# GpSimd adds the identity to the second-next adapter's first tiles one step later, behind the following slot's low parts and mixing matrices

## The reference, cut to what matters

```python
x = x + einsum('bct,bcd->bdt', x, W0[cond])        # x is (32, 64, 1024) f32
x = x + einsum('bct,bcd->bdt', x, W1[cond])        # 64x64 mixings over the sequence
x = x + base(x, W) + low_rank(x, lora[labeler])    # 1024x1024, and rank 32
w = weight[adapter_ids]                            # 8 adapters of 1024x1024, ids 3..7 drawn
x = x + einsum('bsi,boi->bso', x, w)
```

## Time and profile before

| | us |
|---|---|
| median of three runs | 383.75 (383.16 to 384.0) |
| the profiled execution | 384.77 |
| its span, from the first to the last instruction | 383.0 |
| TensorE busy in the span | 376.4 (98%) |
| VectorE busy | 267.6 (70%) |
| ScalarE busy | 225.5 (59%) |
| GpSimd busy | 115.3 (30%) |

### The profile page before, as it was taken

One profiled execution on the slowest core, in us unless ns is written; L12 is line 12 of the kernel. 1 busy time (PEld: TensorE's weight loads), 2 busy tenths in 40 slices (PEclk: granted clock), 3 DMA queues, 4 the chain that ended last, 5 costly groups with the idle time before them and its releaser, 6 DMA issues.

```text
span 383.0 us, 7652 instructions
## 1 busy us (share of the span) xinstructions
PE 376.4 (98%) x1733; PEld 312.9 (82%) x1734; DVE 267.6 (70%) x301; ACT 225.5 (59%) x299; POOL 115.3 (30%) x157
## 2 busy tenths in 40 slices
PE   8999999999999999999999999999999999999995
PEld 7888888888888888888888888778888888888784
DVE  3796977847849788447968458844599635999653
ACT  3689577487247375244474565753677536778443
POOL 0000230100000000024765356663167532566600
PEclk9999999999999999999999999999999999999999
DMA  8975905630378294406528226542256522664223
GB/s 276 399 284 206 344 0 181 236 133 7 106 269 287 103 329 152 171 9 220 159 73 267 63 51 203 205 125 59 56 187 200 169 58 58 205 228 123 60 62 86
DMA packets 24187, 61.38 MB, mean 160 GB/s; under 512 B 1906, under 2 KB 2098, under 8 KB 24114
## 3 DMA queue, kind: packets, MB, share of 16 engines
q1 hardware_dynamic: 23648, 60.10, 47.6%
q10 hardware_dynamic: 466, 0.44, 0.3%
HBM read 52.15 MB, written 8.39 MB: 158 GB/s over the span
## 4 chain that ended last, share of the span: by engine, by line
PE 97%; DMA 1%; issue 0%; DVE 0%; ACT 0%
PE ps L1514 45%; PE ps L1373 12%; PE ps L1374 12%; PE ps L1375 12%; PE ps L1400 4%; PE ps L1537 4%; PE ps L1439 3%; PE ps L1602 2%; PE ps L1412 2%; DMA ring_f<-xt 1%; PE ps L1552 1%; PE ps L1449 0%; DVE ring L878 0%; ACT stage L850 0%
## 5 line engine op out<-in xcount | busy, mean ns | idle before, releaser
L1514 PE MATMUL ps<-ring,aT 128*128 x752 | 173.7, 390 | 0.5 <-issue 0.5
L1514 PEld LDWEIGHTS ps<-ring,aT 128*128 128x128 f32 x752 | 140.9, 188 | 30.8 <-issue 1.7
L1373 PE MATMUL ps<-ring 128*128 128x512 f32 x208 | 81.1, 390 | 0.0
L1374 PE MATMUL ps<-ring 128*128 128x512 f32 x208 | 81.0, 389 | 0.0
L1375 PE MATMUL ps<-ring 128*128 128x512 f32 x208 | 80.9, 389 | 0.0
L476 POOL TENSOR_TENSOR aT<-xT,aT 128x512 fp32r<-128x512 f32 (+1 forms) x36 | 56.4, 1587 | 46.3 <-ACT aT L761 43.1
L1266 DVE TENSOR_TENSOR ring<-raw,ring 128x1024 f32 (+1 forms) x40 | 62.6, 1623 | 6.2 <-ACT ring L747 6.2
L767 ACT ACTIVATE aT<-ps 64x1024 fp32r<-64x1024 f32 x32 | 32.7, 1023 | 47.1 <-PE ps L1514 46.7
L1294 DVE TENSOR_TENSOR stage<-ps,stage 64x1024 f32<-64x1024 f32 x30 | 36.7, 1222 | 29.4 <-ACT stage L776 28.7
L1283 DVE TENSOR_TENSOR aT<-ps,aT 64x1024 fp32r<-64x1024 f32 x32 | 39.1, 1223 | 21.6 <-ACT aT L767 20.9
L1375 PEld LDWEIGHTS ps<-ring 128*128 128x128 f32 x208 | 39.1, 188 | 8.2
(11 more groups left out here) (95 smaller groups left out, 328.6 us busy)
## 6 DMA issues: line engine op xcount, KB each, us to landing
raw<-w3t SPq DMA_DIRECT2D x40, 512.0 KB, 4.4
ring_f<-xt SPq DMA_DIRECT2D x8, 1024.0 KB, 8.4
raw<-xt SPq DMA_DIRECT2D x8, 1024.0 KB, 5.3
out<-stage SPq DMA_DIRECT2D x30, 256.0 KB, 3.2
ring_f<-wt SPq DMA_DIRECT2D x4, 1024.0 KB, 8.1
xT<-xt SPq DMA_DIRECT2D x3, 1024.0 KB, 10.4
xT<-wt SPq DMA_DIRECT2D x2, 1024.0 KB, 16.0
ring_f<-wt SPq DMA_DIRECT2D x4, 256.0 KB, 5.1
```

The lines of the kernel that those rows point to most:

```text
L1373: pe.matmul(dst, hi_of(qw)[:, k, cs], hi_of(qx)[:, k, :], start=start and k == 0, stop=False, skip_group_check=True)
L1374: pe.matmul(dst, hi_of(qw)[:, k, cs], lo_of(qx)[:, k, :], start=False, stop=False, skip_group_check=True)
L1514: last = pe.matmul(acc(i)[:, n, :], x3_split(i, k, start, P), ring[:, bass.ds(off + (part * D + n * 512), 512)], start=(k == 0 and j == 0) ...
```

## The change

In `step` of GpSimd the two kinds of identities are taken apart. Those of MORE, of slot i's word, were added at the end of step i; now they are added in step i+1, behind `slot_lo` of slot i+2 and `mixers` of slot i+1, and ahead of those of LOAD_A of slot i+1. Steps 0 and 1 come to the same order as before with these inputs. No instruction that computes is added or removed, and no other engine's code changes.

```diff
-                for w in ([], [earlier, word])[i] if i < 2 else [word]:
-                    with pool.If(get(w, LOAD_A) > 0):
-                        adapter_eyes(HALF, pool.snap(get(w, THIS)))
-                    with pool.If(get(w, MORE) > 0):
-                        adapter_eyes(0, pool.snap(get(w, THIS) + 1))
+                if i == 1:
+                    with pool.If(get(earlier, LOAD_A) > 0):
+                        adapter_eyes(HALF, pool.snap(get(earlier, THIS)))
+                if i:
+                    with pool.If(get(earlier, MORE) > 0):
+                        adapter_eyes(0, pool.snap(get(earlier, THIS) + 1))
+                    with pool.If(get(word, LOAD_A) > 0):
+                        adapter_eyes(HALF, pool.snap(get(word, THIS)))
                 return word, following
```

## The result

The changed kernel takes 394.31 us (median of six runs, 393.46 to 394.68) against 383.49 us (382.96 to 384.13) for the kernel before: 10.8 us or 2.8% slower, ratio 1.0278, 95% interval 1.0262 to 1.0294. The forecast was 391.6, with a range of 387.5 to 395.0.

What follows compares the result with a forecast made beforehand. TensorE, busy 376.4 of 383.0 us, was taken to bound the kernel. Delays of 1.96 + 2.85 + 3.03 = +7.84 us shift the median from 383.75 to 391.6, range 387.5 to 395.0.

Steps and rivals of the forecast that it cites:

- The bound, and the way: TensorE is busy 376.4 of 383.0 us; a GpSimd change gains only its idle time and can lose by making it wait.
- The chain of the late identities: From T, end of TensorE's slot i-1: late identities delay rows_lo, so mixing starts at T+20.08 instead of T+17.23.
- The choice that mattered: VectorE's four low parts, with GpSimd idle, take 1.25 us each, 5.0 in all, rather than 1.79 each.
- What is given back: At slot 6, slot_lo no longer waits for transfers: 0.55 us hole and 0.34 slow half slot, 0.89 us, once.
- The clock: Behind each hole, mixing and 24 products run at 1.2 instead of 2.4 GHz, 6.35 us more each, 410.6 us; 3%.
- the granted clock stays 1.00: Expected sign in the profile after: TensorE's granted clock does not fall from 1.00.
- if TensorE's products get longer: Sign that the prediction is wrong: TensorE's products take longer than before; no size given.
- a late transfer: A slow transfer puts slot_lo of slot i+2 past its due time by 1 to 2.5 us in a place.
- contention: Low parts at 1.79 us each, or slot_lo of slot i+2 late: 394 to 398 us, chance 8%.
- The second term in the third place: At slot 14's mixing, VectorE goes on without a pause, so that mixing comes 3.03 us later, replacing the 2.85.
- Loads that move with it: Loads of tiles 4 to 7 come later; slot_lo of slot i+2 ends by T+25.7, still fitting before T+26.4.
- Absorbed: VectorE saves 2.1 us beside quiet GpSimd, the chain ends in time, only the hole goes: 382.9 us, chance 5%.

Runs made afterwards that it cites:

- filled kernel: The changed kernel with ten extra throwaway TensorE products ahead of the late mixings of slots 5, 9 and 13: 391.75 us, ratio 1.0213.
- third place alone: The kernel before with the identities of MORE late only for slot 12's word: 387.32 us, ratio 1.0092.
- reordered kernel: The changed kernel with mixed_cols and mixed_sum ahead of the four high and low parts in steps without LOAD_B: 391.25 us, ratio 1.0199.
- kernel after it: The reordered kernel with the identities of tiles 4 to 7 behind the following slot_lo in steps 5 and 9: 389.39 us, ratio 1.0159.
- the first place: The kernel before with the identities of MORE late only for slot 4's word: 386.11 us, ratio 1.0082.

## Why the prediction was right, and where it was off

**The bound, and the way.** Right. TensorE has no slack, the change can only add waits, and it did, ahead of the mixings of slots 5, 9 and 13.

**The chain of the late identities.** Right in every link, and 0.59 us too late at its end: first identity T+7.81 as forecast, first high part T+8.39 for 8.40, first low part T+9.62 as forecast. Two terms were too dear. The four low parts took 4.63, not 5.0, and from `rows_lo` to the mixing it was 0.22, not 0.53. The mixing came at T+19.49 instead of T+20.08, so a hole is 2.26, not 2.85. The choice that mattered, low parts alone and not at 1.79 each, was right. In ScalarE's sum four high parts at 0.98 from T+8.40 end at T+12.3, not T+12.4; nothing hangs on it.

**What is given back.** The step "worth 0.89 us, once" failed. It rested on the single traced execution of the kernel before, and a second one had no hole there. Between those two first traces it can be seen (the shift of the mixing of slot 5 is 1.37, not 2.26), between the medians not. The prediction shifted the median by the same sum as the trace, and this is the wrong place for a hole that three of four traces don't have. How many of the untraced executions have one isn't known.

**The clock.** The rival was right in kind and mis-sized in both chance and price. It had 3% and 6.35 us a place; measured are 0.28, 1.90 and 1.91 us, of which 0.27 each is the slow start of the four mixing products behind any hole. So "the granted clock stays 1.00" is the second step that failed, worth some 3.3 us (4.09 less three times 0.27), of which about 0.25 in the third place is lost at full clock too. The prediction had named "if TensorE's products get longer" as a sign that it is wrong, and by that sign it was: the waits ahead of the mixings were there, if shorter (2.26 for 2.85), but the products behind them got longer. The Trainium skill (TensorE: Matmul & The Clock Gate, HAM oscillation) describes this course, a wait and then a slow start, and the trace agrees in kind: 0.50 behind the hole. The two errors that made the cost too small (0.89 and 4.09) and the one that made it too big (three holes, 8.55 + 0.18 against 6.80) left 7.84 against 10.8. That 394.31 still lies in the range is partly luck: its upper part was there for a late transfer and for contention, and neither made the time.

**The second term in the third place.** The mechanism is there, 12.24 us between the last two late mixings in the filled kernel and 12.37 (351.38 to 363.75) with the third place alone, against 11.8 to 12.0 in the two traces of the kernel before; in the changed kernel itself the slow products hid it.

**Loads that move with it.** The prediction has `slot_lo` of slot 15 end at T+25.7 and says that it fits "with nothing to spare". It ends at T+25.3, and so it was: with the third place alone and full clock there was no hole at slot 15, but the 48 products took 11.12 instead of 10.88. As soon as the mixing came 2 us sooner, slots 7, 11 and 15 waited 0.6 to 2.0 us for just these loads. The waits were real and only covered.

**Absorbed.** The limit named was a first low part at T+6.7. With it at T+7.3 the hole is 0.07. The limit was 0.5 us too strict, by the same two terms as above.

What stays open: why a hole of 2.26 us brings the clock down in one execution and not in another. Its length alone doesn't decide it: behind the wait of 2.01 at slot 15 of the reordered kernel the granted clock was 0.50, and behind the one of 2.97 in the kernel after it 1.00. That the executions of one kernel in the table differ by the clock is read from its mean beside their spans, not from a trace of each; in the first place 386.9 at 0.996 stands above 385.7 at 0.994, so the clock is not all of it.

## What to carry to other kernels

Moving a helper's work behind other work frees what stood behind it and delays what waits for it: before such a move follow the moved result through every queue it enters, down to the engine that bounds the kernel, and count what stands behind it in each. A hole of half a microsecond in one traced execution is no proof of a hole in the median; look at a second execution before paying for its cure. And on a full TensorE a wait can be dearer than its length, and a repair may only uncover the next wait, so read a repair in the idle times of the bounding engine and not in the total alone.

## What was not expected of the hardware

Behind holes of 2.26 us the granted clock fell to 0.50 for about 3 us and took the products with it (1.61 and 12.08 us for 0.91 and 10.88), in some executions and not in others, and one hole of 2.97 us left it at 1.00; with ten throwaway products in each hole it stayed at 1.00. Even at full clock the first four products behind a hole took 1.18 us instead of 0.91. That part doesn't depend on the length of the hole: behind waits of 0.07 us it was 1.19.
